# Graph convolutions of a four-layer graph network: table lookups by TensorE removed, every column gathered by GpSimd

## The chip, the core and the metric

One Trainium2 chip, one core of it. The time is the device time of one execution of the whole kernel, in microseconds (us). The kernel before takes 32684.31 us, the median of 3 runs (32668.05 to 32695.04).

## What is computed

Four graph layers run one after the other on 12500 nodes with 16 features and 400000 edges, sorted by destination: graph attention (two passes), a graph convolution network, a sheaf layer and a tensor-product layer. Each adds its result to `x` and normalises. The change touches the second layer, which aggregates over the edges twice:

```
def gcn_conv(x, edge_index, W, b, num_nodes):
    src, dst = (edge_index[0], edge_index[1])
    ...
    deg = segment_sum(ones, dst_f)
    dinv = where(deg > 0, rsqrt(deg), 0.0)
    norm = dinv[src_f] * dinv[dst_f]
    h = x @ W
    msg = h[src_f] * norm[:, None]
    out = segment_sum(msg, dst_f)
    return out + b

h = gcn_conv(x, edge_index, W1, b1, num_nodes)      # 16 -> 32 features
h = relu(batch_norm(h))
out = gcn_conv(h, edge_index, W2, b2, num_nodes)    # 32 -> 16 features
x = layernorm(x + out)
```

## The kernel before

The 400000 edges lie in 128 lanes of 3125 edges, one lane to a partition, and are worked in 25 chunks of 125 columns (`CH`). A column is one edge of each lane, so one column needs 128 rows of a node table, each at an index of its own. Nodes lie as 100 columns of 128 (`NT`).

Both aggregations of the graph convolution work on 16 features (the product with the weights stands after the first one and before the second), in the function `gcn_gather` (L935). Its two calls have the names `c1c` and `c2c`, made by `aggregate` in `gcn` (L2163 to L2171). Values are scaled by `dinv` and stored to a table in HBM (`tab16`, `tab16b`), and then, per chunk:

- **GpSimd** gathers columns 0 to 84 (`PCH` = 85) with one indirect DMA per column, 128 rows of 64 bytes, from the table into `G[b]`, one of two buffers (L494 in `gather_column_loop`). Ahead of a chunk it waits until the buffer was stored and the chunk's indices have landed, and then issues column after column without a wait.
- **TensorE and VectorE** look up columns 85 to 124 (`PC` = 40), ten batches of 4 columns (`NB`, `BE`), in the class `Match` (L1209). For a batch VectorE makes 13 one-hot masks of 128x512 (`heat`, L1269: is this index in this piece of the table), TensorE multiplies each mask with the piece of the table, in two parts for precision (L1278), VectorE keeps the right 16 of 128 rows (`mask`, L1288), TensorE sums them (`collapse`, L1298), and VectorE copies the result to `G` (`empty`, L1306). The indices of those columns were written once to HBM as numbers of two kinds by `match_rows` (L1169) at the start of the program; SyncE's queue loads them, spread over all partitions, 20 DMAs of 128 KB per chunk (L1258).
- Beside that a **side task** runs (`count_before_group`, L1074), which the sheaf layer needs later: 11 groups of 5 columns per chunk in `c1c`, 10 in `c2c`. Of each, VectorE makes two one-hot tiles (L1097, L1099), compares (`loT`, L1102), waits for TensorE's lookup (`pR`, L1127), and then multiplies, reduces and adds (L1105, L1107, L1108). ScalarE copies one 128x100 tile per group.
- At the end of a chunk VectorE waits for the gathered columns and runs 16 scans of 125 columns over `G` (L975), copies the last column to `carry` (L978), and SyncE loads the indices of the chunk after next (L501) and stores `G` to HBM (L1017).

The order on VectorE within a chunk is written by hand: masks of batch 0, then for each step `m` the `mask` of batch m-1, the masks of batch m+1, the side group m, and the `empty` of batch m-1. The last two groups have no masks ahead of them. The loop over chunks is a hardware loop over pairs of chunks with the last one behind it.

Elsewhere in the program the same `gather_column_loop` runs with all 125 columns: in the attention layer (`g1g_G`, `g2g_G`) beside other VectorE work, and in the sheaf layer (`se_G`). `extract` (L427) issues 4 times 25 indirect DMAs of the same kind behind each aggregation, with little beside them.

## Time and profile before

| | |
|---|---|
| median of 3 runs | 32684.31 us (32668.05 to 32695.04) |
| the profiled execution | 32672.44 us, its span 32670.6 us |
| busy, share of the span | PE 41%, PEld 32%, DVE 49%, ACT 8%, POOL 69% |
| stage `c1c`, from the first gather to the last scan | 11322 to 14779 us |
| stage `c2c` | 15144 to 18569 us |

DVE is VectorE, ACT ScalarE, POOL GpSimd, SP SyncE (SPq its DMA queue), PE TensorE's matmuls and PEld its weight loads. Times in the rows below are counted from the start of the span. A duration of a `DMA_INDIRECT` row is the time in which GpSimd issues the transfer, not that in which the data move. An idle time that ends by "issue" is one in which the engine waited for nothing that the profile shows.

### The profile page before, as it was taken

Reading aid. Unit: us, or ns where it says so; the run is one execution under the profiler, and the core shown is the slowest. Engines: PE = TensorE matmul, PEld = TensorE weight load, DVE = VectorE, ACT = ScalarE, POOL = GpSimd, SP = SyncE. Lnnn points to the kernel's source line nnn. Section 1 sums busy time; section 2 is a strip of 40 time slices with the busy share of each in tenths; the row PEclk is TensorE's granted clock in tenths of the full one; section 3 lists DMA queues with packets and bytes.
Section 4 is the critical chain, followed back from the end, with each engine's and each line's share of the span. In section 5 each row is a group of like instructions: output and inputs, shape, how many; then the busy total and the mean of one; then the engine's idle time right before and its main releaser. Section 6 shows DMA issues by size and latency. Waiting matters only on the chain. (4 is left out here: it accounts for less than half of the span.)

```text
span 32670.6 us, 266258 instructions
## 1 busy us (share of the span) xinstructions
PE 13491.3 (41%) x71326; PEld 10479.5 (32%) x71326; DVE 16103.5 (49%) x34560; ACT 2584.3 (8%) x3901; POOL 22511.4 (69%) x20275
## 2 busy tenths in 40 slices
PE   1111100211110177775777535444444441666663
PEld 1111100211110166664666423232323230454442
DVE  3434429344443677775777534444444443444442
ACT  0000000000000000000000001011111110333330
POOL 5777760477775288885888767777777774777772
PEclk5555555555555588886888756666666665777775
DMA  2111113111112311111111110000000002000001
GB/s 55 16 15 16 16 10 145 22 27 27 27 27 46 111 33 33 33 32 21 33 33 33 25 15 12 14 12 14 12 14 12 14 10 59 18 15 15 15 13 56
DMA packets 1117655, 946.20 MB, mean 29 GB/s; under 512 B 609084, under 2 KB 1060308, under 8 KB 1092308
## 3 DMA queue, kind: packets, MB, share of 16 engines
q1 hardware_dynamic: 468516, 706.27, 7.3%
q0 software_dynamic: 646368, 201.76, 6.4%
q10 hardware_dynamic: 1872, 28.29, 0.2%
q8 instruction: 307, 5.03, 0.1%
q14 instruction: 592, 4.85, 0.1%
HBM read 506.74 MB, written 428.17 MB: 29 GB/s over the span
## 5 line engine op out<-in xcount | busy, mean ns | idle before, releaser
L494 POOL DMA_INDIRECT g1g_G<-tab,g1g_stage x3125 | 3270.3, 1046 | 1237.8 <-issue 1025.7
L494 POOL DMA_INDIRECT se_G<-tab,se_stage x3125 | 3324.5, 1064 | 1085.3 <-issue 1072.5
L494 POOL DMA_INDIRECT g2g_G<-tab,g2g_stage x3125 | 2949.5, 944 | 1272.5 <-issue 1026.4
L1152 POOL DMA_INDIRECT messages<-pe_M,pe_rstage x2625 | 3178.9, 1211 | 905.3 <-issue 817.5
L1152 POOL DMA_INDIRECT messages<-se_M,se_rstage x2625 | 2980.1, 1135 | 865.7 <-issue 799.6
L494 POOL DMA_INDIRECT c2c_G<-tab16b,c2c_stage x2125 | 2769.4, 1303 | 856.0 <-issue 647.3
L494 POOL DMA_INDIRECT c1c_G<-tab,c1c_stage x2125 | 2761.3, 1299 | 793.7 <-issue 647.3
L1053 DVE SCALAR_TENSOR_TENSOR g2gh_junk<-g2gh_pB,g2gh_src_f,earlier 128x128 f32<-128x128 f32 (+4 forms) x2625 | 1453.7, 614 | 1951.3 <-POOLq L493 1928.0
L1567 PE MATMUL se_pTV<-ident,se_pair 128*32 128x128 f32 x3125 | 539.5, 313 | 4159.9 <-DVE se_pair L1474 4159.4
L739 PE MATMUL g1gh_acc<-g1gh_oh_hi,g1gh_oh_lo 128*128 128x100 bf16 x6250 | 539.0, 283 | 3746.7 <-DVE g1gh_oh_hi L719 3746.7
L1065 PE MATMUL g2gh_pB<-ident_b,src_lo 128*128 128x128 bf16 x2625 | 641.4, 286 | 3290.3 <-DVEq L1059 3249.5
L1278 PE MATMUL c1cm_acc<-c1cm_hot,c1cm_part 128*128 128x512 f32 x6500 | 1740.7, 429 | 344.3 <-DVE c1cm_hot L1269 344.3
L1278 PE MATMUL c2cm_acc<-c2cm_hot,c2cm_part 128*128 128x512 f32 x6500 | 1717.2, 425 | 400.9 <-DVE c2cm_hot L1269 400.9
L1567 PEld LDWEIGHTS se_pTV<-ident,se_pair 128*32 128x32 f32 x3125 | 283.8, 106 | 4534.9 <-issue 4486.2
L739 PEld LDWEIGHTS g1gh_acc<-g1gh_oh_hi,g1gh_oh_lo 128*128 128x128 bf16 x6250 | 508.6, 143 | 3777.1 <-DVE g1gh_oh_hi L719 3777.1
L717 DVE TENSOR_TENSOR g1gh_oh_lo<-dst_lo,iota 128x640 bf16<-128x640 f32 (+1 forms) x625 | 514.6, 823 | 2284.6 <-POOLq L493 2231.8
L1473 DVE COPY se_pair<-se_G 128x80 f32 (+1 forms) x625 | 139.9, 224 | 2888.7 <-DMA se_G<-tab,se_stage 2761.6
L1278 PEld LDWEIGHTS c1cm_acc<-c1cm_hot,c1cm_part 128*128 128x128 f32 x6500 | 1356.2, 213 | 640.7 <-issue 336.7
L1278 PEld LDWEIGHTS c2cm_acc<-c2cm_hot,c2cm_part 128*128 128x128 f32 x6500 | 1338.2, 210 | 691.3 <-issue 389.2
L1787 DVE TENSOR_TENSOR pe_outer<-pe_X,pe_A 128x640 f32 x625 | 520.9, 833 | 1941.8 <-PE pe_pT L1815 1855.5
L1065 PEld LDWEIGHTS g2gh_pB<-ident_b,src_lo 128*128 (+1 forms) x2625 | 278.4, 106 | 3433.3 <-issue 3187.5
L1822 PE MATMUL pe_pM<-p_wm,pe_outT 128*128 128x16 f32 x6250 | 905.2, 283 | 1034.6 <-ACT pe_outT L1849 1034.6
(607 smaller groups left out, 34105.5 us busy)
## 6 DMA issues: line engine op xcount, KB each, us to landing
scans<-g1w_W SPq DMA_DIRECT2D x25, 3187.5 KB, 10.0
c1cm_row<-match SPq DMA_DIRECT2D x500, 128.0 KB, 3.0
c2cm_row<-match SPq DMA_DIRECT2D x500, 128.0 KB, 3.0
edges<-g2g_G SPq DMA_DIRECT2D x25, 2062.5 KB, 6.8
g2w_G<-edges SPq DMA_DIRECT2D x25, 2062.5 KB, 11.6
scans<-g2w_W SPq DMA_DIRECT2D x25, 2062.5 KB, 7.3
g1g_G<-tab,g1g_stage POOLq DMA_INDIRECT x3125, 2.4
g2g_G<-tab,g2g_stage POOLq DMA_INDIRECT x3125
```

The costliest lines, as they stand in the source:

```text
L494: g.indirect_dma_start(out=G[b][:, t, :], out_offset=None, in_=table, in_offset=bass.IndirectOffsetOnAxis(ap=stage[b][:, t:t + 1], axis=0) ...
L717: v.tensor_tensor(oh_lo[o][b][:, part, :], bc(lo[:, at], [P, m, P], 2), bc(k.iota[:, :], [P, m, P], 1), ALU.is_equal).then_inc(ready, 1)
L739: mm = pe.matmul(acc[2 if o and direct else o][:, 0:NT], oh_lo[o][b][:, g, :], oh_hi[o][b][:, g, :], start=False, stop=True, skip_group_ch ...
L1053: ins = v.scalar_tensor_tensor(out=junk[g][:, :], in0=pB[b][:, a * GRP * P:(e + 1) * P], scalar=src_f[:, e:e + 1], in1=k.earlier[:, (GRP - ...
L1065: pe.matmul(pB[b][:, e * P:(e + 1) * P], k.src_lo[:, at].to_broadcast([P, P]), k.ident_b[:, :], start=True, stop=False)
L1152: g.indirect_dma_start(out=view, in_=M[b][:, DC + t, :], in_offset=None, out_offset=bass.IndirectOffsetOnAxis(ap=stage[b][:, t:t + 1], axis=0)
L1278: mm = pe.matmul(self.acc[m % 2][:, :], self.part[part][:, j * MR:(j + 1) * MR, :].rearrange("p r f -> p (r f)"), self.hot[m % 2][:, j, :] ...
L1473: ch(v.tensor_copy(pair[:, :, 0, :], G[b][:, at, 0:D]))
L1567: mm = pe.transpose(pT[:, g * P:(g + 1) * P], pair[:, g, :, :].rearrange("p n d -> p (n d)"), k.ident[:, :])
L1787: v.tensor_tensor(outer[:, :, :, :], bc(X[b][:, at, :], [P, GRP, D, DE], 3), bc(A[b][:, at, :], [P, GRP, D, DE], 2), ALU.mult).then_inc(ou ...
L1822: mm = pe.matmul(pM[:, g * D:(g + 1) * D], outT[:, g * P:(g + 1) * P], w[:, :], start=True, stop=True)
```

## The change

`gcn_gather` no longer uses `Match`. GpSimd gathers all 125 columns of a chunk, and SyncE's queue loads 125 indices per lane instead of 85. Gone are: the masks, `mask` and `empty` on VectorE, `multiply` and `collapse` on TensorE, the 20 loads of match rows per chunk on SyncE's queue, the preparation of the table's two parts (`vector_first`), and `match_rows` at the program's start. The side task, the scans and the stores stand as before. The line numbers of the functions behind the cut constants are 7 lower in the changed kernel up to `gcn_gather`.

```diff
--- before.py
+++ after.py
@@ -43,13 +43,6 @@
 XT = 25
 FULL, REST = N // P, N % P
 D = 16
-BE = 4
-PC = 40
-PARTS, PART_T = 2, mybir.dt.float32r
-NB = PC // BE
-PCH = CH - PC
-MR = P // D
-MJ = -(-NT // MR)
 H1, C1 = 3, 32
 C2 = 32
 HID = 64
@@ -932,45 +925,33 @@
                 over_chunks(a, chunk)
 
 
-def gcn_gather(k, name, table, values, left, scans, carry, side):
+def gcn_gather(k, name, table, scans, carry, side):
 
     with ExitStack() as st:
         c = Ctx(k.nc, st)
         G = [c.sb(f"{name}_G{b}", [P, CH, D]) for b in range(2)]
-        stage = [c.sb(f"{name}_stage{b}", [P, PCH], I32) for b in range(2)]
+        stage = [c.sb(f"{name}_stage{b}", [P, CH], I32) for b in range(2)]
         staged = [c.sem(f"{name}_staged{b}") for b in range(2)]
         got = [c.pool_dma_sem(f"{name}_got{b}") for b in range(2)]
         stored = [c.sem(f"{name}_stored{b}") for b in range(2)]
         scanned, step = c.sem(name + "_scanned"), c.sem(name + "_step")
         side = side(k, c, name + "h")
-        match = Match(k, c, name + "m", left)
         with k.nc.Block() as block:
             @block.gpsimd
             def _(g):
                 over_chunks(g, lambda i, b, j: gather_column_loop(
-                    g, i, j, b, table, G, stage, staged, stored, 16, got, PCH))
+                    g, i, j, b, table, G, stage, staged, stored, 16, got))
 
             @block.vector
             def _(v):
                 ch = Chain(v, step)
                 ch(v.memset(carry[:, 0:D], 0.0))
-                match.vector_first(v, ch, values)
                 side.vector_first(v)
 
                 def chunk(i, b, j):
-                    match.heat(v, i, 0)
-                    v.wait_ge(stored[b], (j + 1) * 16)
-                    for m in range(max(NB + 1, side.groups)):
-                        if 1 <= m <= NB:
-                            match.mask(v, i, m - 1)
-                        if m + 1 < NB:
-                            match.heat(v, i, m + 1)
-                        if m < side.groups:
-                            side.vector(v, ch, i, side.ranges[0][0] + m)
-                        if 1 <= m <= NB:
-                            match.empty(v, G[b], i, m - 1)
-                    v.wait_ge(match.emptied, (i + 1) * NB + 2)
-                    v.wait_ge(got[b], (j + 1) * (16 * PCH))
+                    for m in range(side.groups):
+                        side.vector(v, ch, i, side.ranges[0][0] + m)
+                    v.wait_ge(got[b], (j + 1) * (16 * CH))
                     for f in range(D):
                         ch.loose(v.tensor_tensor_scan(G[b][:, :, f], k.keep_d[:, cols(i)], G[b][:, :, f],
                                                       carry[:, f:f + 1], ALU.mult, ALU.add))
@@ -982,19 +963,12 @@
 
             @block.tensor
             def _(pe):
-                match.tensor_first(pe)
                 side.tensor_first(pe)
 
                 def chunk(i, b, j):
-                    for m in range(max(NB + 1, side.groups)):
-                        if m < side.groups:
-                            side.tensor_rows(pe, i, side.ranges[0][0] + m)
-                        if m < NB:
-                            match.multiply(pe, i, m)
-                        if 1 <= m <= NB:
-                            match.collapse(pe, i, m - 1)
-                        if m < side.groups:
-                            side.tensor(pe, i, side.ranges[0][0] + m, False)
+                    for m in range(side.groups):
+                        side.tensor_rows(pe, i, side.ranges[0][0] + m)
+                        side.tensor(pe, i, side.ranges[0][0] + m, False)
                 over_chunks(pe, chunk)
 
             @block.scalar
@@ -1005,24 +979,19 @@
             def _(s):
                 for b in range(2):
                     s.sem_inc(stored[b], 16)
-                    load_indices(s, k.src_lanes, stage, staged, b, b, 0, PCH)
-
-                def chunk(i, b, more=True, index=True):
+                    load_indices(s, k.src_lanes, stage, staged, b, b)
+
+                def chunk(i, b, more=True):
+                    s.wait_ge(scanned, i + 1)
                     if more:
-                        for m in range(NB):
-                            match.reload(s, i, m)
-                    s.wait_ge(scanned, i + 1)
-                    if index:
-                        load_indices(s, k.src_lanes, stage, staged, i + 2, b, 0, PCH)
+                        load_indices(s, k.src_lanes, stage, staged, i + 2, b)
                     s.dma_start(rows(scans)[:, cols(i), :], G[b][:, :, :]).then_inc(stored[b], 16)
-                for m in range(NB):
-                    match.load(s, 0, m)
                 with s.Fori(0, PAIRS - 1) as j:
                     chunk(2 * j, 0)
                     chunk(2 * j + 1, 1)
                 chunk(NCH - 3, 0)
-                chunk(NCH - 2, 1, True, False)
-                chunk(NCH - 1, 0, False, False)
+                chunk(NCH - 2, 1, False)
+                chunk(NCH - 1, 0, False)
                 s.wait_ge(stored[0], 16 * (PAIRS + 2))
                 s.wait_ge(stored[1], 16 * (PAIRS + 1))
 
@@ -1164,147 +1133,6 @@
                 s.dma_start(k.rank_lanes.rearrange("p (i c) -> p i c", c=CH)[:, :, DC:CH],
                             k.rank[:, :].rearrange("p (i c) -> p i c", c=CH)[:, :, DC:CH]).then_inc(stored, 16)
                 s.wait_ge(stored, 16)
-
-
-def match_rows(k, name):
...
-class Match:
...
 class DirectSums:
@@ -1907,7 +1735,6 @@
         k.lanes = k.dram("lanes", [P, 51])
         k.spread_buf = k.dram("spread_buf", [SPREAD_SIZE])
         scan16 = k.dram("scan16", [E + P, D])
-        k.match = [k.dram(f"match{h}", [NCH, PC * P], F16) for h in range(2)]
         k.carried = k.dram("carried", [P + 1, 51])
         tab16 = k.dram("tab16", [NP, D])
         tab16b = k.dram("tab16b", [NP, D])
@@ -1925,7 +1752,6 @@
                 k.dst_i = Ctx(nc, s0).sb("dst_i", [P, LANE], I32)
                 setup(k, x, src, dst)
                 digits(k, "ds", k.src_i, k.src_lo, k.src_hi)
-            match_rows(k, "mr")
             with ExitStack() as s2:
                 k.h2 = Ctx(nc, s2).sb("h2", [P, NT, C2 + 2])
                 gat1(k, w, dst, carry, first, y)
@@ -2165,7 +1991,7 @@
             vector_block(k, name + "a", lambda v, ch: ch(v.tensor_tensor(
                 xs[:, :, :], values, bc(dinv[:, :], [P, NT, D], 2), ALU.mult)))
             store_nodes(k, name + "b", [xs[:, :, :]], table)
-            gcn_gather(k, name + "c", table, xs[:, :, :], agg, scan16, carry, side)
+            gcn_gather(k, name + "c", table, scan16, carry, side)
             lane_carries(k, name + "d", carry[:, 0:D], D, k.by_dst, ALU.add, scan16)
             extract(k, name + "e", scan16, k.by_dst, agg, D, ALU.add)
 
```

On VectorE, at the start of the first loop over chunks of `c1c`. The one-hot masks and `kept` belong to `Match`, the other rows to the side task. Before, without rows that only set registers:

```order
L1269 TENSOR_SCALAR c1cm_hot<-c1cm_row,c1cm_first 128x512 x13
...
L1097 TENSOR_TENSOR c1ch_oh_lo<-src_lo,iota 128x640
...
L1099 TENSOR_TENSOR c1ch_oh_hi<-src_hi,iota 128x500
...
L1102 TENSOR_SCALAR c1ch_loT<-c1ch_pB,part 128x640
L1105 TENSOR_TENSOR c1ch_prod<-c1ch_pR,c1ch_oh_hi 128x500
...
L1107 TENSOR_REDUCE c1ch_r<-c1ch_prod 128x5
...
L1108 TENSOR_TENSOR rank<-c1ch_r,rank 128x5
...
L1288 SCALAR_TENSOR_TENSOR c1cm_kept<-c1cm_row,c1cm_slot,c1cm_acc 128x512
L1269 TENSOR_SCALAR c1cm_hot<-c1cm_row,c1cm_first 128x512 x13
```

and now:

```order
L1066 TENSOR_TENSOR c1ch_oh_lo<-src_lo,iota 128x640
...
L1068 TENSOR_TENSOR c1ch_oh_hi<-src_hi,iota 128x500
...
L1071 TENSOR_SCALAR c1ch_loT<-c1ch_pB,part 128x640
L1074 TENSOR_TENSOR c1ch_prod<-c1ch_pR,c1ch_oh_hi 128x500
...
L1076 TENSOR_REDUCE c1ch_r<-c1ch_prod 128x5
...
L1077 TENSOR_TENSOR rank<-c1ch_r,rank 128x5
```

The groups of the side task now follow each other with nothing between them.

On GpSimd, the whole of the gather of `c1c`: the loop body with two chunks, and the last chunk behind it. Before:

```order
L93 ISA
L494 DMA c1c_G<-tab,c1c_stage 128x16 x170
L93 REGISTER_ALU
L93 COMPARE_AND_BRANCH
L494 DMA c1c_G<-tab,c1c_stage 128x16 x85
```

and now:

```order
L86 ISA
L487 DMA c1c_G<-tab,c1c_stage 128x16 x250
L86 REGISTER_ALU
L86 COMPARE_AND_BRANCH
L487 DMA c1c_G<-tab,c1c_stage 128x16 x125
```

Nothing else was moved between these rows; a pair of chunks now has 250 indirect DMAs in place of 170.

## Rows read from the trace of the kernel before

**Rows 1.** Groups of instructions: busy us, mean ns of one, idle before, releaser
```profile
L494 POOL DMA_INDIRECT g1g_G<-tab,g1g_stage x3125 | 3270.3, 1046 | 1237.8 <-issue 1025.7 <-DMA g1g_stage<-in_src_dram 212.1
...
L494 POOL DMA_INDIRECT g2g_G<-tab,g2g_stage x3125 | 2949.5, 944 | 1272.5 <-issue 1026.4 <-DMA g2g_stage<-in_src_dram 246.1
L494 POOL DMA_INDIRECT c2c_G<-tab16b,c2c_stage x2125 | 2769.4, 1303 | 856.0 <-issue 647.3 <-DMA c2c_stage<-in_src_dram 208.7
L494 POOL DMA_INDIRECT c1c_G<-tab,c1c_stage x2125 | 2761.3, 1299 | 793.7 <-issue 647.3 <-DMA c1c_stage<-in_src_dram 146.4
...
L717 DVE TENSOR_TENSOR g1gh_oh_lo<-dst_lo,iota 128x640 bf16<-128x640 f32 (+1 forms) x625 | 514.6, 823 | 2284.6 <-POOLq L493 2231.8 <-issue 47.4 <-DVE carry L817 4.6
...
L719 DVE TENSOR_TENSOR g1gh_oh_hi<-dst_hi,iota 128x500 bf16<-128x500 f32 (+1 forms) x625 | 419.6, 671 | 0.0
```

**Rows 2.** Waits in stage c1c: total us, times, longest us
```profile
POOL c1c_G L494 <- issue: 647.3, 2124, 0.3
DVE c1ch_prod L1105 <- PE c1ch_pR L1127: 622.6, 275, 5.2
```

**Rows 3.** Tiles c1c_G, then c2c_G: min/median/max ns, first and last start us
```profile
L494 POOL DMA_INDIRECT c1c_G<-tab,c1c_stage x2125: 940/947/8802, 11322.2 to 14729.9; - x194
L978 DVE COPY carry<-c1c_G x25: 174/176/383, 11467.5 to 14778.6; 128x16 f32<-128x16 f32 x25
L494 POOL DMA_INDIRECT c2c_G<-tab16b,c2c_stage x2125: 940/947/8406, 15144.2 to 18560.0; - x194
L978 DVE COPY carry<-c2c_G x25: 174/175/386, 15294.6 to 18568.4; 128x16 f32<-128x16 f32 x25
```

**Rows 4.** Timeline of c1c where masks are made: start us, us, instruction
```profile
12021.21 10.44 DVE L1269 TENSOR_SCALAR c1cm_hot<-c1cm_row,c1cm_first 128x512 fp32r<-128x512 f16 x26 [0.22 <-DVE carry L978]
12024.17 7.61 POOL L494 DMA_INDIRECT c1c_G<-tab,c1c_stage  x1 [0.31 <-issue]
...
12044.71 0.82 DVE L1097 TENSOR_TENSOR c1ch_oh_lo<-src_lo,iota 128x640 bf16<-128x640 f32 x1
12045.22 1.72 POOL L494 DMA_INDIRECT c1c_G<-tab,c1c_stage  x1 [0.30 <-issue]
```

**Rows 5.** Timeline of c1c, a group without masks, then the scans
```profile
12144.91 0.84 DVE L1097 TENSOR_TENSOR c1ch_oh_lo<-src_lo,iota 128x640 bf16<-128x640 f32 x1
12145.68 0.67 DVE L1099 TENSOR_TENSOR c1ch_oh_hi<-src_hi,iota 128x500 bf16<-128x500 f32 x1
12146.15 1.02 POOL L494 DMA_INDIRECT c1c_G<-tab,c1c_stage  x1 [0.30 <-issue]
...
12151.88 6.03 DVE L975 TENSOR_TENSOR_SCAN c1c_G<-keep_d,carry,c1c_G 128x125 f32<-128x125 f32 x16
12153.82 1.18 POOL L494 DMA_INDIRECT c1c_G<-tab,c1c_stage  x1 [0.30 <-issue]
```

**Rows 6.** Windows without masks, POOL's gathers alone: 8 of c1c, 5 of c2c, summed
```profile
sum 133.50, POOL 102.22; mean POOL 12.78
sum 24.80, POOL 19.04; mean POOL 3.81
```

**Rows 7.** Windows, stages c1c and g1g: us, busy (x) by engine, PEclk, DMA share, GB/s
```profile
11320.00:14780.00 3460.00, 2605.36 (x14002) 2257.45 (x14002) 2711.07 (x5834) 69.92 (x276) 2761.33 (x2125) 0.82 0.16 32
...
215.00:4510.00 4295.00, 539.45 (x6253) 508.77 (x6253) 1737.60 (x2623) 0.00 (x0) 3268.90 (x3124) 0.53 0.13 22
```

**Rows 8.** Timeline of GpSimd in the extraction behind c1c, 23 columns in a row
```profile
14811.40 0.94 POOL L427 DMA_INDIRECT c1e_gs<-scan,c1e_si  x1 [0.30 <-issue]
...
14838.88 0.94 POOL L427 DMA_INDIRECT c1e_gs<-scan,c1e_si  x1 [0.30 <-issue]
```

**Rows 9.** Timeline, the last gather of stage c2c
```profile
18559.97 0.94 POOL L494 DMA_INDIRECT c2c_G<-tab16b,c2c_stage  x1 [0.30 <-issue]
```

**Rows 10.** Timeline of VectorE, first instruction of match_rows and first behind it
```profile
43.41 1.20 DVE L1190 CAST mr_src_f<-src_i 128x1000 f32<-128x1000 int32 x1 [0.52 <-PEq L305]
...
69.96 0.14 DVE L1987 MEMSET g_w1d<- 48x96 f32 x1 [6.20 <-remote]
```

118 lines of the change are left out of this document (removed).

## The prediction

> **What bounds the kernel now.** The stages run one after the other, so only the two gathers of the graph convolution and `match_rows` can move by themselves. I read the groups of instructions first, then the waits inside stage `c1c`, then its timeline.
>
> The first thing to see is that GpSimd hardly rests in either gather. Its 2125 gathers of `c1c` are busy 2761.3 us, and every gap between two of them is "issue", 0.3 us at most [rows 1, 2]. It runs from 11322.2 to about 14730.8, in 3409 us [rows 3]. VectorE ends its last chunk at 14778.6, with a period of (14778.6 - 11467.5)/24 = 138.0 us per chunk against GpSimd's 3409/25 = 136.4 [rows 3]. So before the change the two sides of the stage are level: VectorE, which also waits 622.6 us for TensorE's lookup [rows 2], is ahead as the bound by under 2 us per chunk.
>
> The second thing is that GpSimd's 85 columns are not cheap there. One gather is 1299 to 1303 ns in these stages, 944 ns in `g2g` [rows 1]. The timeline shows the cause: a gather that falls beside 26 back-to-back masks takes 7.61 us, and one beside the one-hot tile behind 13 masks takes 1.72 us [rows 4]. The median is 947 ns, the maximum 8802 [rows 3]; a few gathers pay for all. Per chunk the excess is (1299 - 944) x 85 = 30 us.
>
> **What a column costs without the masks.** The clean rate: 22 columns that follow each other in the extraction take 14838.88 - 14811.40 = 27.48 us, 1.249 us each [rows 8], which is 0.944 of issue and 0.304 of gap (647.3/2124) [rows 2]. The same 0.944 stands over 3125 gathers of `g2g` [rows 1].
>
> On top comes what the remaining VectorE work takes. Beside `oh_hi` and `loT` a gather takes 1.02 us, beside the scans 1.18 us [rows 5]. Over 16 groups without masks of `c1c`, 133.5 us, GpSimd is busy 102.22: the idle 31.28 at 0.304 are 103 columns, whose clean issue would be 97.1, so 5.1 us are excess, 0.32 per group. Over five groups of `c2c` the same working gives 5.76/0.304 = 18.9 columns, 17.9 clean, 1.15 of excess, 0.23 per group [rows 6]. The third source agrees: `g1g` has 50 pairs of such tiles per chunk and (1046 - 944) x 125 = 12.8 us of excess, 0.26 per pair [rows 1]. The 16 scans run 6.03 us and stretch some three gathers by 0.24 each [rows 5]: 0.7 us.
>
> Per chunk that makes 11 x 0.32 + 0.7 = 4.2 us in `c1c` and 10 x 0.23 + 0.7 = 3.0 us in `c2c`, on top of 125 x 1.249 = 156.1.
>
> **The change part by part.**
> - Gathers, `c1c`: GpSimd starts at 11322.2 as before (the first index load has 125 instead of 85 columns, no matter). 3125 x 1.249 = 3903 and 25 x 4.2 = 105 bring it to 15330. The end of the stage lies behind the last gather: in `c2c` before, it ended at 18559.97 + 0.94 and the copy to `carry` at 18568.4 + 0.17, 7.7 us later [rows 3, 9]. So 15338, against 14778.7: **+559 us**.
> - Gathers, `c2c`: 15144.2 + 3903 + 75 + 7.7 = 19130, against 18568.6: **+561 us**.
> - Masks, `mask`, `empty`, `multiply`, `collapse`, the preparation of the table and 500 loads of match rows per stage: nothing of it stands on the new critical path, which is GpSimd alone. Its only worth there is that the gathers run cleanly again, and that is in the rate above. VectorE's share of a chunk falls to the side groups and the scans. A group without masks is 6.97 us from its `oh_lo` to the scans [rows 5], with `kept` and `empty` still in it, so a chunk is 11 x 7 + 6.5 = 84 us, beside 160 us of gathering. That is the cover of the side task: 76 us per chunk to spare. SyncE's queue loses its waits for `kept`; index load and store then wait only for `scanned`, a chunk ahead of when GpSimd wants them, some 150 us.
> - `match_rows` goes: VectorE's first instruction of it starts at 43.41, the next stage's at 69.96, nothing beside it [rows 10]: **-26.5 us**.
> - Between the stages nothing changes in kind.
>
> Sum: 559 + 561 - 26.5 = +1094 us on the profiled execution's 32672, so 33766. The median of the runs stands 12 us above that execution; against it I forecast **33770 us**, 3.3% slower.
>
> **Ends of the range.** What I don't know is the excess on 125 columns when side groups follow each other. Its lowest value is none (the rate of `g2g`), 180 us less: 33590. Its highest near value is that each group costs what one does behind the masks, 1.72 - 0.94 = 0.78 us [rows 4]: 11 x 0.78 + 0.7 = 9.3 per chunk, 5.1 more than priced, over 50 chunks 255 us more: 34020. A gain is excluded for this term, since the minimum of all 2125 gathers is 940 ns [rows 3]. I take the values in between because three stretches without masks agree on 0.23 to 0.32. Range: 33590 to 34020.
>
> **A rule weighed.** In `g1g` the one-hot tiles occupy VectorE for some 2 x (514.6 + 419.6) = 1868 us (the pair of `dst` and the like pair of `src`), 75 us per chunk, and cost the gathers 12.8 us [rows 1]: 0.17 us per us of such work, not one for one. Per side group, 1.49 us of tiles give 0.25. The Trainium skill (SBUF — State Buffer, "SBUF: two separate sides") calls the port pair that VectorE and GpSimd share an exclusive lock, held for the whole instruction by a VectorE instruction in a two-port mode or with two SBUF inputs, while the other is fully blocked. By that rule the sum would be that of rival 2, 34670, instead of 33770. For the masks it points the right way (the 7.61 us gather [rows 4]); for the tiles it is too dear by the rows.
>
> **Rivals.**
> 1. *The excess per column of `g1g` holds.* There VectorE makes tiles all the time, and a column costs 0.102 us over the clean issue; it would be 12.8 us per chunk instead of 3.0 to 4.2, 640 in place of 180: 34230. For it: both are the same tiles and the same 125 columns. Against it: 100 tiles per chunk there, 20 to 22 here. 5%.
> 2. *Tiles and scans block GpSimd for their whole length.* 11 x 1.49 + 6.0 = 22.4 and 10 x 1.49 + 6.0 = 20.9 us per chunk, 1083 in place of 180: 34670. Against it stand the scans of 6.03 us, beside which gathers still come out in 1.18 [rows 5], and the 75 us of tiles per chunk of `g1g` that cost 12.8 [rows 1]. 3%. (It is the lock of the Trainium skill's SBUF page, taken literally.)
> 3. *The side task becomes the bound.* TensorE's granted clock is 0.82 in `c1c` and 0.53 in `g1g`, where it has less to do [rows 7]; near 0.5 it works at the lower of its two levels, 1.2 GHz, and each group would wait longer for `pR`. The longest such wait now is 5.2 us, the mean 622.6/275 = 2.3 [rows 2]. From 14 us per group on, twice today's 7, a chunk of `c1c` would pass 160 us; at 15 it would be 171.5 and the kernel 285 us slower than forecast, 34055. 2%.
> 4. *The other side: the gathers get cheaper than clean.* Issue might today wait for the DMA engines, which 20 loads of 128 KB per chunk on SyncE's queue share with it. The kernel comes out not slower only when a column costs under 1.249 - 1094/6250 = 1.074 us. If a quarter of the 0.944 went, a column would be 1.013 and the kernel 6250 x 0.236 = 1475 us faster than forecast, 32295. Against it: with no such load about, in the extraction and in `g2g`, issue is 0.94 all the same [rows 1, 8]. 1%.
>
> **Chances.** The forecast with its range has 0.88; the rivals 0.05, 0.03, 0.02 and 0.01; 0.01 is left for what I don't see. All but the fourth end over 0.2% slower (about what a measurement of this kernel can tell from no change). So slower 0.98, within 0.2% 0.01, faster 0.01. The range leaves out rivals 1, 2 and 4 and little else.
>
> **What would show each step.** In the groups: `c1c_G` and `c2c_G` with 3125 gathers each at 965 to 985 ns and no row of `c1cm_` or `c2cm_`. In the tiles: the maximum of a gather under 2 us, a span of about 4008 us in `c1c` and 3978 in `c2c`. In the waits: VectorE's largest wait of the stage is for the gather's DMA, 25 times some 75 us; GpSimd waits only for "issue". In the windows: TensorE's clock at 0.5 to 0.6. Wrong would be: gaps of GpSimd that end by a store or an index load (the buffers bound it); gathers beside `oh_lo` and `oh_hi` of over 2 us (rivals 1 and 2); VectorE with no wait for the gather at a chunk's end (rival 3); gathers under 900 ns (rival 4).

## The result: 4.3% slower, and the profile after

The changed kernel takes **34096.87 us** (median of 4 runs, 34084.25 to 34101.07) against 32686.44 (32668.05 to 32695.04) for the kernel before: ratio 1.0432 [1.0414, 1.045]. The forecast was 33770, its range 33590 to 34020. Direction and bound were right; 327 us were missing.

The groups of the changed kernel, costliest first (busy us, mean ns of one, idle before and its releaser); line numbers are the changed kernel's:

```profile
L487 POOL DMA_INDIRECT g1g_G<-tab,g1g_stage x3125 | 3276.7, 1049 | 1208.9 <-issue 1025.4 <-DMA g1g_stage<-in_src_dram 183.5
...
L487 POOL DMA_INDIRECT c1c_G<-tab,c1c_stage x3125 | 3110.3, 995 | 1170.3 <-issue 1024.6 <-DMA c1c_stage<-in_src_dram 145.8
L487 POOL DMA_INDIRECT c2c_G<-tab16b,c2c_stage x3125 | 3079.1, 985 | 1233.4 <-issue 1024.7 <-DMA c2c_stage<-in_src_dram 208.7
```

They answer to [rows 1]. A gather is down from 1299 and 1303 ns to 995 and 985, now that the masks, beside which [rows 4] had the dearest, are gone. There are 1000 more of them per stage. The idle time by "issue" is 1024.6 over 3124 gaps, 0.328 each, where [rows 2] had 0.305.

The tile `c1c_G`, then `c2c_G` (min/median/max ns, first and last start), against [rows 3]:

```profile
L487 POOL DMA_INDIRECT c1c_G<-tab,c1c_stage x3125: 938/944/1557, 11300.8 to 15434.8; - x196
L959 DVE COPY carry<-c1c_G x25: 174/175/176, 11471.6 to 15443.3; 128x16 f32<-128x16 f32 x25
L487 POOL DMA_INDIRECT c2c_G<-tab16b,c2c_stage x3125: 938/944/1547, 15806.5 to 19909.4; - x196
L959 DVE COPY carry<-c2c_G x25: 174/175/384, 15977.1 to 19917.8; 128x16 f32<-128x16 f32 x25
```

The waits of stage `c1c` (total us, times, longest), against [rows 2]:

```profile
DVE c1c_G L956 <- DMA c1c_G<-tab,c1c_stage: 2088.8, 25, 91.8
POOL c1c_G L487 <- issue: 1024.6, 3124, 3.3
DVE c1ch_prod L1074 <- PE c1ch_pR L1096: 699.5, 275, 2.6
```

GpSimd alone bounds the stage: VectorE waits 84 us per chunk for the gathers, GpSimd never waits for a buffer. But one thing is new in that view: the longest wait by "issue" was 0.3 us, and now is 3.3. The windows of both stages, columns as in [rows 7], show TensorE at a granted clock of 0.50 and 0.51, its lower level of 1.2 GHz, with nothing on the path:

```profile
11300.00:15445.00 4145.00, 935.28 (x5495) 857.85 (x5495) 1204.80 (x2074) 69.58 (x275) 3110.35 (x3125) 0.50 0.09 13
15806.00:19920.00 4114.00, 850.16 (x4995) 779.95 (x4995) 1109.55 (x1924) 63.25 (x250) 3079.14 (x3125) 0.51 0.09 13
```

**Two costs that the sum lacked or had too small** are seen in the timeline of `c1c` (start us, us, instruction). First, GpSimd at the 113th and 114th gather of a chunk:

```profile
12107.01 0.94 POOL L487 DMA_INDIRECT c1c_G<-tab,c1c_stage  x1 [0.31 <-issue]
12108.25 0.94 POOL L487 DMA_INDIRECT c1c_G<-tab,c1c_stage  x1 [0.30 <-issue]
12112.35 0.94 POOL L487 DMA_INDIRECT c1c_G<-tab,c1c_stage  x1 [3.15 <-issue]
12113.60 0.94 POOL L487 DMA_INDIRECT c1c_G<-tab,c1c_stage  x1 [0.30 <-issue]
```

Each of the 25 chunks has exactly one such gap, of 3.1 to 3.3 us, ahead of its 114th gather. It is no property of the change: the kernel before has it in its three gathers of 125 columns, 25 times in each. Second, two side groups that follow each other, with the gathers between them:

```profile
12141.83 0.82 DVE L1066 TENSOR_TENSOR c1ch_oh_lo<-src_lo,iota 128x640 bf16<-128x640 f32 x1 [0.24 <-DVE rank L1077]
12141.96 1.51 POOL L487 DMA_INDIRECT c1c_G<-tab,c1c_stage  x1 [0.30 <-issue]
12142.57 0.67 DVE L1068 TENSOR_TENSOR c1ch_oh_hi<-src_hi,iota 128x500 bf16<-128x500 f32 x1
...
12148.63 0.83 DVE L1066 TENSOR_TENSOR c1ch_oh_lo<-src_lo,iota 128x640 bf16<-128x640 f32 x1 [0.24 <-DVE rank L1077]
12148.77 1.50 POOL L487 DMA_INDIRECT c1c_G<-tab,c1c_stage  x1 [0.30 <-issue]
```

The groups come every 6.80 us, and each one's `oh_lo` starts 0.13 us ahead of a gather, which then takes 1.50 us. Five clean gathers take 5 x 1.249 = 6.245 us; with 0.55 of excess they take the same 6.80. Where groups follow each other VectorE's period is 6.80 us all along (median 6.803), and the gathers fall into step with it; why is told below, with e16. In the kernel before, [rows 5] had one group without masks behind masks, at a phase of its own.

Where the time went, trace against trace (us, from starts and lengths in the timelines):

| stretch | before | after | difference | forecast |
|---|---|---|---|---|
| start to first gather of `c1c` | 11322.2 | 11300.8 | -21.4 | -26.5 |
| `c1c`, first gather to end of last copy to `carry` | 3456.6 | 4142.6 | +686.1 | +559 |
| between the two | 365.5 | 363.1 | -2.4 | 0 |
| `c2c`, the same | 3424.3 | 4111.4 | +687.1 | +561 |
| all behind it | 14102.0 | 14173.9 | +71.9 | 0 |

The five differences sum to the spans' 34091.9 - 32670.6 = 1421.3.

### The profile page after: what moved, and what is told of

Same layout as the page of the kernel before. It is cut to its first block and busy times, and to the rows that moved or that the text cites. A ratio compares the mean times of both kernels' runs of the same rounds, so it can differ in the third digit from the quotient of the medians.

```text
span 34091.9 us, 220370 instructions
## 1 busy us (share of the span) xinstructions
PE 10210.6 (30%) x54301; PEld 7718.8 (23%) x54301; DVE 13094.5 (38%) x27031; ACT 2583.6 (8%) x3901; POOL 23222.9 (68%) x22275
## 5 line engine op out<-in xcount | busy, mean ns | idle before, releaser
L487 POOL DMA_INDIRECT c2c_G<-tab16b,c2c_stage x3125 | 3079.1, 985 | 1233.4 <-issue 1024.7
L487 POOL DMA_INDIRECT c1c_G<-tab,c1c_stage x3125 | 3110.3, 995 | 1170.3 <-issue 1024.6
L1096 PE MATMUL c1ch_pR<-c_free_place,c1ch_loT 128*128 128x100 f32 x2750 | 674.1, 432 | 3116.3 <-DVE c1ch_loT L1071 3116.3
L1096 PE MATMUL c2ch_pR<-c_free_place,c2ch_loT 128*128 128x100 f32 x2500 | 613.0, 432 | 3164.8 <-DVE c2ch_loT L1071 3164.8
L1096 PEld LDWEIGHTS c1ch_pR<-c_free_place,c1ch_loT 128*128 128x128 f32 x2750 | 606.0, 329 | 3189.4 <-DVE c1ch_loT L1071 3189.4
L1096 PEld LDWEIGHTS c2ch_pR<-c_free_place,c2ch_loT 128*128 128x128 f32 x2500 | 551.0, 329 | 3231.1 <-DVE c2ch_loT L1071 3231.1
L1650 PEld LDWEIGHTS pe_pM<-p_wm,pe_outT 128*128 128x128 f32 x6250 | 894.3, 219 | 1326.4 <-ACT pe_outT L1677 1246.6
```

The lines of the kernel that those rows point to most:

```text
L487: g.indirect_dma_start(out=G[b][:, t, :], out_offset=None, in_=table, in_offset=bass.IndirectOffsetOnAxis(ap=stage[b][:, t:t + 1], axis=0) ...
L1096: mm = pe.matmul(pR[:, g * NT:(g + 1) * NT], loT[:, g, :], table[:, :], start=True, stop=True)
L1650: mm = pe.matmul(pM[:, g * D:(g + 1) * D], outT[:, g * P:(g + 1) * P], w[:, :], start=True, stop=True)
```

## The experiments

Sixteen runs of twelve kernels stand here; four are repeats on another chip or a second time, and two are the kernels before and after as they are. Letters name theories: **S**, the gap belongs to more than 113 gathers in a row on one semaphore; **A**, it belongs to a run of gathers without a wait; **L**, the excess per group comes from the step between groups and gathers, not from the amount of VectorE's work; **M**, the stages behind got slower because buffers moved in HBM. The runs e1 to e10 fell on a chip on which VectorE, TensorE and ScalarE stood still for tens of us at a time (ScalarE for up to 56) in every trace, and the kernel before took 39.3 ms in place of 32.7. So their times say nothing on GpSimd's costs, and only gaps and durations are read from them. The runs e11 to e17 fell on two others. There the kernel before took 32549 us beside e11 to e13 and 32693 beside e14 to e17; the changed kernel took 34097 beside 32686 and 34099 beside 32549, so its variants are set against those two. It was not run on the chip of e14 to e17, and why the kernel before differs by 144 us from chip to chip, where the changed one doesn't, is open.

### Where the gap comes from

**e1_wait_mid** and **e2_wait_early**: a wait, already fulfilled, in the middle of the gathers of `c1c` and `c2c`.

```diff
     for t in range(count):
+        if pause is not None and t == pause:      # 63 in e1, 8 in e2
+            g.wait_ge(staged[b], (j + 1) * 16)
+            g.nop(nofuse=True)
```

Expected of e1: 

> In the changed kernel every chunk of 125 gathers has one gap of 3.1 to 3.3 us ahead of its 114th gather, where the others are 0.305. Here one wait that is met already (for the chunk's indices, again) and a nop stand ahead of the 64th gather of each chunk of both graph convolution stages. Theory A, the gap comes of more than 113 gathers in a row without a wait: all 50 gaps go, both stages get 25 x 2.9 = 72 us shorter (the waits themselves cost under 0.2 us each), and the kernel 135 to 145 us shorter than the changed kernel's 34097, near 33955. Theory B, the gap comes of the place in the code (an instruction fetch) or of something that counts on over chunks: the gaps stay, at the same or another place, and the time stays within 20 us.

Expected of e2: 

> As the run with a wait in the middle of a chunk, but the wait stands ahead of the 9th gather, so that 117 gathers follow it. Theory A (a count since the last wait of GpSimd): the gap stays but moves by 8, ahead of the 122nd gather of a chunk, and the time is that of the changed kernel. If the count began at the chunk's start or at the loop's, the gap stays ahead of the 114th. If any wait at all in a chunk removed it, it would be gone and both stages 72 us shorter.

41475.22 us (ratio 1.052 [1.0454, 1.0587]) and 41213.48, beside 39393.83 for the kernel before. The gap stays ahead of the 114th gather, 25 times per stage, in both. A falls. The attention layer's gathers, which have one more semaphore instruction every 5 columns, have it there too. From e1, the 113th and 114th gather of a chunk:

```profile
15056.13 0.94 POOL L490 DMA_INDIRECT c1c_G<-tab,c1c_stage  x1 [0.30 <-issue]
15060.18 0.94 POOL L490 DMA_INDIRECT c1c_G<-tab,c1c_stage  x1 [3.10 <-issue]
```

**e4_cols85**: only columns 0 to 84 are gathered; the other 40 are left out (zeros stand in `G`).

```diff
-                    g, i, j, b, table, G, stage, staged, stored, 16, got))
+                    g, i, j, b, table, G, stage, staged, stored, 16, got, 85))
```

Expected: 

> Leaves out the gathers of columns 85 to 124 of both graph convolution stages (those columns are zeroed once and not looked up in any way), so the output is not the reference's. Theory, the stage is the sum of its gathers: no long gap (85 is under 113), a chunk takes 85 x 1.249 plus the excess by VectorE, which the changed kernel shows as 6.4 us in c1c and 5.1 in c2c, so 112.6 and 111.3 us per chunk and 2816 and 2782 us from the first gather on. Against the 136.4 of the kernel before, with as many gathers, that is what the masks cost GpSimd: 24 us per chunk. Rival, the side task bounds a chunk once the gathers are short: VectorE would have no wait for the gather at a chunk's end, and the period would be 84 us or more by its own work; at 112 us it should still wait some 30 us per chunk.

39281.28 us. No gap inside any chunk; the only long ones are at chunk starts, where GpSimd waits for the store of the buffer, which stands behind VectorE's chunk end (848.5 us in `c1c`). So the gap needs more than 85 gathers. The expected 112.6 us per chunk can't be judged here: this chip's VectorE bounds the stage.

**e7_reversed**: the columns are issued from 124 down to 0.

```diff
-    for t in range(count):
+    for t in (reversed(range(count)) if back else range(count)):
```

Expected: 

> A wait in the middle or near the start of a chunk left the long gap of GpSimd (3.2 us) ahead of the 114th gather, so it is no count since the last wait and, as the code had grown by two instructions, no fixed place in the code. Here the 125 columns of a chunk of both graph convolution stages are gathered from the last to the first. Theory C, the gap belongs to the operand (column 113 of the index tile or of the buffer): it moves ahead of the 13th gather issued. Theory E, it is a count of gathers since the chunk began: it stays ahead of the 114th issued. Times as for the changed kernel in both cases.

40742.9 us (before 39298.81). The gap is ahead of the 114th gather issued, column 11, and not of column 113: it goes by the count, not by the operand.

**e8_two_sems**: columns 0 to 62 count on one semaphore, 63 to 124 on a second one, in `c1c` and `c2c`; VectorE waits for both.

```diff
-                             ).then_inc(got[b], 16)
+                             ).then_inc((late if late and t >= 63 else got)[b], 16)
...
-                    v.wait_ge(got[b], (j + 1) * (16 * CH))
+                    v.wait_ge(got[b], (j + 1) * (16 * 63))
+                    v.wait_ge(late[b], (j + 1) * (16 * (CH - 63)))
```

Expected: 

> The first 63 gathers of a chunk count up one semaphore, the other 62 a second one, in both graph convolution stages; VectorE waits for both. Theory S, the gap comes of more than 113 gathers in a row on one semaphore: it goes, 25 gaps in each stage, and each stage is 72 us shorter than in the changed kernel (4143 and 4112 us from first gather to the last copy to carry). If the count is of gathers whatever their semaphore, the gap stays ahead of the 114th and the times stay.

40953.32 us. The gaps are gone from both stages, and stay in the three gathers left as they were. S holds: 125 gathers on one semaphore have the gap, 85 don't, and 63 and 62 on two don't. GpSimd's instructions are the same in number and order, so their place in the code is not it either.

**e11_after_all_sems** has that edit in all five gathers, **e12_after_again** is the changed kernel itself, for the same chip.

Expected of e11: 

> The changed kernel with columns 63 to 124 of every chunk on a second semaphore in all five gathers. Theory S (the gap comes with more than 113 gathers in a row on one semaphore, and is on the path of the stages that GpSimd bounds): no gap of over 1 us inside a chunk in any of the five; the two convolution gathers each 60 to 75 us shorter than in the unaltered changed kernel, the two of the attention layer by up to as much where GpSimd bounds them, the sheaf layer's not at all; 130 to 290 us in all. Rival (the gap lies beside a wait for VectorE at the chunk's end anyway on this chip): gap gone, time within 60 us of the unaltered one.

Expected of e12: 

> The changed kernel itself, unaltered, on the chip on which its variants ran, so that they have it to be set against. No theory hangs on it alone. By the stages of its trace: GpSimd's gap of 3.1 to 3.3 us ahead of the 114th gather in each of the 25 chunks of both convolution gathers; a period of 6.80 us and an excess of 0.50 to 0.55 us where side groups follow each other (phase lock). If it shows neither, both are properties of the variants and not of the change. Time: between 40700 and 41300 us on this chip, from the variants with one edit each (40743 to 41213).

e12: 34098.73 us (34091.6 to 34146.29), ratio 1.0474 [1.0456, 1.0491] to the kernel before. e11: 33727.11 (33714.81 to 33732.01), ratio 1.0361 [1.0343, 1.0378]; **372 us less** than e12, and more than the 130 to 290 expected. (e12's own time was expected at 40700 to 41300, for the chip of e1 to e10; it has the gap and the step as expected.) The groups of e11:

```profile
L487 POOL DMA_INDIRECT c1c_G<-tab,c1c_stage x3125 | 3113.3, 996 | 1097.9 <-issue 952.1 <-DMA c1c_stage<-in_src_dram 145.8
L487 POOL DMA_INDIRECT c2c_G<-tab16b,c2c_stage x3125 | 3089.5, 989 | 1160.7 <-issue 952.1 <-DMA c2c_stage<-in_src_dram 208.6
```

The gathers are as long as ever, and the idle time by "issue" is down from 1024.6 to 952.1: 72.5 us, which is 25 x 2.9. That is the cost of the gap per stage. It was expected of four stages; the sheaf layer's gather, of which nothing was expected, took 7858 us and had taken 7939 in the changed kernel's first trace, 81 more. Its gathers and scatters follow each other on GpSimd, so it is on the path there as well. Five stages of 72.5 us make 363; e11 also has shorter turns in the product layer (27 us, see below), so the sum fits only roughly.

### What the step between groups and gathers costs

**e5_pad**, its repeat **e5b_pad**, and on the other chip **e16_pad_alone**: one more copy on VectorE per side group, whose result is not used. More work makes the period longer, 7.52 us, near six clean gathers (7.49).

```diff
         ch(v.tensor_reduce(r5[:, :], prod[:, :, :], axis=AX.X, op=ALU.add))
+        ch(v.tensor_copy(pad[:, 0:500], pR[:, 0:500]))
```

Expected of e5: 

> Adds one VectorE copy of 128x500 from PSUM to SBUF, about 0.7 us, to every side group of both stages; it reads no SBUF tensor. In the changed kernel a group takes 6.8 us and meets five gathers, 5 x 1.249 = 6.25; the trace shows nearly every group's one-hot tile starting just behind the start of a gather, which takes 1.5 us instead of 0.94. Theory L, the two engines are locked in step: the excess per group is what is missing between the group's length and a whole number of gathers, 0.55. With 7.5 us per group, six gathers (7.49) fit, the excess falls to 0.1 or less, and both stages get shorter by about 11 x 25 x 0.4 = 110 and 10 x 25 x 0.35 = 90 us, though work was added. Theory F, a one-hot pair costs a fixed 0.5 us whatever its place: the stages stay as they are within 15 us. Theory H, more VectorE work means more excess: they get longer.

Expected of e5b: 

> The kernel with one VectorE copy from PSUM of 0.7 us more in each side group, again, since the chip of its first run held VectorE and TensorE up for some 27 us at a time in every kernel, which hid what was asked. As then: theory L (the engines are locked in step; a group of 7.5 us fits six gathers) says an excess of 0.1 us or less per group and stages about 110 and 90 us shorter than the changed kernel's 4143 and 4112; theory F (a fixed 0.5 us per one-hot pair) says no change within 15 us; theory H says longer.

Expected of e16: 

> The changed kernel with one more VectorE copy of 128x500 per side group, from the accumulator in PSUM to SBUF; what it computes is not used. Theory L (the groups run in step with the gathers, so that each group's first tile falls on the start of a gather): period 7.52 us, six gathers, excess per group about 0.1 us in place of 0.55 and 0.47; that is 11 x 0.45 + 10 x 0.37 = 8.7 us for the two convolutions' chunks together, 25 x 8.7 = 215 us off the changed kernel's 34099, to about 33880, although VectorE does more. Rival (the excess comes from the amount of VectorE work): no gain, or slower than 34099.

e5: 41928.95 us, ratio 1.0635 [1.0532, 1.0739]; e5b: 41933.31, 1.067 [1.0484, 1.0856]; in both the mean gather is 953 to 955 ns. That proves little: on that chip, e1, e2, e7 and e8 without the copy had 970 to 982 in `c1c` and 956 to 958 in `c2c`, and the stages did not get shorter as expected, since VectorE bounded them. e16 gives the time: **33854.94 us** (33849.65 to 33869.1), 244 less than e12, ratio 1.0359 [1.0343, 1.0375]. Its groups, and two groups' starts in its timeline:

```profile
L487 POOL DMA_INDIRECT c1c_G<-tab,c1c_stage x3125 | 2992.5, 958 | 1169.8 <-issue 1024.0 <-DMA c1c_stage<-in_src_dram 145.8
L487 POOL DMA_INDIRECT c2c_G<-tab16b,c2c_stage x3125 | 2986.6, 956 | 1233.3 <-issue 1024.6 <-DMA c2c_stage<-in_src_dram 208.7
```

```profile
12335.78 0.68 DVE L1078 COPY c1ch_pad<-c1ch_pR 128x500 f32<-128x500 f32 x1
...
12336.99 0.88 DVE L1067 TENSOR_TENSOR c1ch_oh_lo<-src_lo,iota 128x640 bf16<-128x640 f32 x1 [0.24 <-DVE rank L1079]
12337.01 0.94 POOL L487 DMA_INDIRECT c1c_G<-tab,c1c_stage  x1 [0.30 <-issue]
12337.79 0.67 DVE L1069 TENSOR_TENSOR c1ch_oh_hi<-src_hi,iota 128x500 bf16<-128x500 f32 x1
12338.26 1.02 POOL L487 DMA_INDIRECT c1c_G<-tab,c1c_stage  x1 [0.30 <-issue]
...
12344.56 0.89 DVE L1067 TENSOR_TENSOR c1ch_oh_lo<-src_lo,iota 128x640 bf16<-128x640 f32 x1 [0.24 <-DVE rank L1079]
12344.59 0.94 POOL L487 DMA_INDIRECT c1c_G<-tab,c1c_stage  x1 [0.30 <-issue]
...
12777.11 0.94 POOL L487 DMA_INDIRECT c1c_G<-tab,c1c_stage  x1 [0.30 <-issue]
12777.68 0.82 DVE L1067 TENSOR_TENSOR c1ch_oh_lo<-src_lo,iota 128x640 bf16<-128x640 f32 x1 [0.24 <-DVE rank L1079]
12778.36 0.96 POOL L487 DMA_INDIRECT c1c_G<-tab,c1c_stage  x1 [0.30 <-issue]
```

L holds. The busy time of the gathers falls by 117.8 us in `c1c` and 92.5 in `c2c`, 210 together, where 215 were expected; the rest of the 244 lies behind these stages, which the edit doesn't touch (the sheaf gather takes 7910 us in place of 7939). The same tiles cost 0.08 us (1.02 - 0.94) where the gather starts 0.02 to 0.03 us behind `oh_lo`, and 0.56 where it starts 0.13 behind it. In the first case `oh_lo` itself takes 0.88 in place of 0.82 and the groups come every 7.57 us; in most groups of e16 the period is 7.52 us, a gather starts 0.57 ahead of `oh_lo` and the next one takes 0.96 or 0.97, as in the last three rows. The excess in step is what is left of VectorE's period over whole gathers: 6.80 - 5 x 1.249 = 0.56 there, 7.52 - 6 x 1.249 = 0.03 here.

Why they fall into step is seen in the changed kernel's trace, where now and then a gather starts later beside the tiles:

```profile
11803.69 0.82 DVE L1066 TENSOR_TENSOR c1ch_oh_lo<-src_lo,iota 128x640 bf16<-128x640 f32 x1 [0.26 <-DVE carry L959]
11804.31 1.03 POOL L487 DMA_INDIRECT c1c_G<-tab,c1c_stage  x1 [0.30 <-issue]
11804.43 0.67 DVE L1068 TENSOR_TENSOR c1ch_oh_hi<-src_hi,iota 128x500 bf16<-128x500 f32 x1
...
12303.32 0.82 DVE L1066 TENSOR_TENSOR c1ch_oh_lo<-src_lo,iota 128x640 bf16<-128x640 f32 x1 [3.13 <-issue]
12303.56 1.40 POOL L487 DMA_INDIRECT c1c_G<-tab,c1c_stage  x1 [0.30 <-issue]
12304.06 0.67 DVE L1068 TENSOR_TENSOR c1ch_oh_hi<-src_hi,iota 128x500 bf16<-128x500 f32 x1
```

These gathers start 0.62 and 0.24 us behind `oh_lo`, those in step 0.13, and all end 1.64 or 1.65 us behind its start, 0.23 us behind the end of `oh_hi`. In that trace it is so for all 456 gathers of both stages that start 0.07 to 0.66 us behind `oh_lo` (0.22 to 0.24 us behind the end of `oh_hi`). So such a gather is held until `oh_hi` is done, and where it ends no longer hangs on where it began. From that end the next starts can be counted: the gap and four clean gathers bring the next one beside tiles to 1.64 + 0.30 + 4 x 1.249 - 6.80 = 0.14 us behind the next `oh_lo`, where it is held again. With the period of e16 and five clean gathers it is 1.64 + 0.30 + 5 x 1.249 - 7.52 = 0.67 us (0.68 in the last row of e16 above), so late that hardly anything of `oh_hi` is left to wait for.

**e10_all_sems_pad** and, on the other chip, **e17_all_sems_pad**: both edits in the changed kernel.

Expected of e10: 

> The changed kernel with both finds: two semaphores per chunk in all five gathers of 125 columns, and the VectorE copy of 0.7 us more per side group of the graph convolutions. Theories S and L together: 125 x 2.9 = 363 us and some 11 x 25 x 0.44 + 10 x 25 x 0.37 = 213 us off the changed kernel's 34097, so 33520, a ratio to the kernel before of 1.026; the five stages have no gap over 0.4 us within a chunk, the gathers of both graph convolutions 952 ns or less. That is still slower than before, since 2000 gathers more at 1.249 us are 2498 us and the lookups that they replace took as long as the gathers beside them. Without L (a fixed price per one-hot pair): 33730.

Expected of e17: 

> Both edits in the changed kernel: second semaphore in all five gathers and the extra copy per side group. If the two costs are separate terms they add: 371 us (measured for the semaphores alone) and 215 us (expected for the copy alone), so about 33510, still slower than the kernel before by about 3%, since 80 more columns of GpSimd at 1.249 us in each pair of chunks remain. Rival (they overlap): over 33600.

e10: 42032.84 us, ratio 1.0687 [1.06, 1.0773]: no gain to be seen, since VectorE bounded the stages there (GpSimd waits 1576 us for the store of its buffer in `c1c`). e17: **33462.86 us** (33452.12 to 33470.66), ratio 1.024 [1.0225, 1.0256], 636 less than e12; the single edits gave 372 and 244, together 616. From the first gather to the last, `c1c` and `c2c` are 132 us shorter in e11 than in the changed kernel's first trace, 211 in e16 (together 343) and 360 in e17. So the two costs are separate terms and add.

### The stages behind, and a version that beats both

**e13_dram_kept**: the changed kernel with the removed lookup's HBM buffers still laid out.

```diff
+        k.match = [k.dram(f"match{h}", [NCH, 40 * P], F16) for h in range(2)]
```

Expected: 

> The changed kernel with the two HBM buffers of the removed lookup (k.match) still laid out and never used, so that every buffer behind them lies at the address it had before the change. Theory M (what is behind the second convolution got 72 us longer because its tables and scans moved in HBM): the scatter of the sheaf layer and its matrix products are back near 1135 and 594 ns, and from the last gather of the second convolution to the end of the span it takes some 70 us less than in the unaltered kernel of the same call. Rival (it is the clock or the instruction layout): no difference beyond the scatter between two executions of one kernel. Gathers and gaps of the convolution unchanged in both.

34092.73 us, ratio 1.0472 [1.0455, 1.049]: 6 us from e12, inside its runs. The scatter of the sheaf layer takes 1150 ns. M falls.

**e14_before_again**: the kernel before, a second trace.

Expected: 

> The kernel before, unaltered, for a second trace of it. Open is why everything behind the second convolution took 72 us longer in the changed kernel. If that belongs to the change, the sheaf gather takes 7891 us and the rest 5820 again, with a mean of 1135 ns for the sheaf layer's scatter and 407 us of waits for its one-hot tiles. Rival (one execution differs so from another): 7920 or more and 1145 ns or more.

32705.12 us, with 1136 ns for that scatter. The rows of the sheaf layer's scatter, of e14 and of the changed kernel:

```profile
L1152 POOL DMA_INDIRECT messages<-se_M,se_rstage x2625 | 2982.7, 1136 | 865.4 <-issue 799.6 <-DVE se_M L1533 65.8
```

```profile
L1121 POOL DMA_INDIRECT messages<-se_M,se_rstage x2625 | 3022.8, 1152 | 865.0 <-issue 799.6 <-DVE se_M L1361 65.4
```

Two traces of the one kernel against three of the other (1150 to 1161 ns) say that the difference belongs to the program and not to one execution. From the first gather of the sheaf layer to its last it takes 7891 and 7893 us in two traces of the kernel before, 7939, 7963 and 7944 in three of the changed one. Some 40 us of it are these scatters; what stretches them is not shown. In e16, whose edit is in the convolution alone, they take 1139 ns, nearly as before the change. In the product layer behind it, GpSimd's idle time at every second turn of a chunk, where the hardware loop turns, is 4.7 to 5.2 us after the change and 2.5 before. Eleven turns make some 27 us:

```profile
28324.87 1.23 POOL L1152 DMA_INDIRECT messages<-pe_M,pe_rstage  x1 [2.52 <-issue]
```

```profile
29728.95 2.79 POOL L1121 DMA_INDIRECT messages<-pe_M,pe_rstage  x1 [5.18 <-issue]
```

(the first of the kernel before, the second of the changed one, the first of these turns in each). In e11 and e17 that idle time is back at 2.5, although they only change semaphores; in e12, e13 and e16 it is not. So it goes with the build. What of a build sets it was not found, and no further kernel was tried for it.

**e9_before_two_sems**, and **e15_before_two_sems** on the other chip: the kernel before with the second semaphore in its three gathers of 125 columns.

Expected of e9: 

> The kernel before, with its lookups by TensorE, and the semaphore changed after 63 of 125 gathers in the three stages that gather all 125 columns (both attention gathers and the sheaf layer). Theory S (a long gap of 3.2 us once more than 113 gathers in a row count up one semaphore) says: 25 gaps of each of the three stages go, 75 x 2.9 = 218 us, and the kernel comes to 32470 us where the kernel before takes 32686, a ratio of 0.993; where another engine ends the chunk, less. If the gaps were hidden, the ratio is 1.000.

Expected of e15: 

> The kernel before with columns 63 to 124 of the 125-column gathers (both of the attention layer and the sheaf layer's) on a second semaphore, once more. On a chip whose VectorE and TensorE are not held up, by theory S: both attention gathers 60 to 75 us shorter and, as the changed kernel with the same edit showed, the sheaf gather about 80 shorter; 200 to 220 us in all, so 0.993 to 0.994 of the kernel before, which would beat both kernels. Rival (the convolution stages, which VectorE bounds by a hair, take it back): there is no coupling between stages, so none of it should be lost; a ratio above 0.997 would speak for this.

e9: 39152.54 us, ratio 0.9956 [0.9918, 0.9994], where 0.993 was expected. e15: **32536.89 us** (32528.06 to 32543.41) against 32693.02 (32641.96 to 32697.93) for the kernel before, ratio 0.9956 [0.9942, 0.9969]. It is 0.4% faster than the kernel before on the same chip, the only version that is, though 156 us are less than the 200 to 220 expected. Its waits in `g2g`:

```profile
POOL g2g_G L494 <- issue: 952.1, 3124, 0.3
```

The two attention gathers gave 54 and 75 us against e14, about as expected. The sheaf gather gave 25 in place of 80: its gaps by "issue" fell by 54 us, but its scatter rose from 1136 to 1146 ns, 26 us.

## Why the prediction was wrong in size and right in kind

The measured 34096.87 lies 77 us above the range. The steps that failed are terms of the sum: the gap per gather, sized at 0.304 us and 0.328 in fact; the excess per side group, sized at 0.32 and 0.23 us and 0.55 and 0.47 in fact; and the stages behind, put at nothing, where 72 us came. None of the four rivals came; this was the 0.01 left for what was not seen, where the range had been given 0.88.

**Held.** GpSimd is the only bound of both stages; VectorE waits 25 times for the gather (84 and 89 us, forecast "some 75"); TensorE's clock is at 0.50; the longest gather is 1.56 us, under 2; no row of `Match` is left; the minimum of a gather is 938 ns, nothing cheaper than clean. The gathers of `c1c` were forecast at 965 to 985 ns and take 995; `c2c`'s take 985. The buffers never made GpSimd wait.

**Failed, by their steps.**

1. *"The clean rate: ... 1.249 us each", times 125.* The rate was read over 22 columns in a row and the gap of 0.304 over chunks of 85. In chunks of 125 the mean gap is 0.328. The missing 2.9 us per chunk are 72 us per stage, 145 in all; e11 showed 72.5 in each. The number stood in [rows 1]: `g1g` and `g2g`, with 125 columns, have 1025.7 and 1026.4 us of "issue", 0.328 per gap, and the waits of `c1c` have 647.3/2124 = 0.305 [rows 2]. I took `g2g`'s 0.944 as the like case and its gap from another.
2. *"0.32 per group" and "0.23 per group".* Both came from groups without masks behind masks. Groups that follow each other cost 0.55 in `c1c` and 0.47 in `c2c`, since they are in step with the gathers. The scans, priced at 0.7, cost 0.9 (four gathers in place of three). The mean gathers give 125 x (995 - 944) = 6.4 and 125 x (985 - 944) = 5.1 us per chunk in place of 4.2 and 3.0: +54 and +53 us. Groups behind the scans, which are not in step, cost 0.2 on average (0.23 and 0.22) in the changed kernel, near the figures read. The upper end of 0.78 would have covered this term alone. (Redone with `c2c`'s own numbers that end is 34035, which changes nothing.)
3. *"Between the stages nothing changes in kind."* True up to `c2c` (-2.4), but behind it the kernel is 72 us slower, by the two places above. This had no range at all.
4. *`match_rows`, -26.5.* It gave 21.4: 5 us.

The four make 145 + 107 + 72 + 5 = 329, less the 2 between the stages: the missing 327. The end of the range, 34020, held 255 us for step 2 and nothing for 1 and 3. That the direction came out is no luck: 2000 more gathers at 1.249 us on an engine that was level with the bound before; the 127 and 126 us missing per stage change the size and not the sign.

**The rivals.** The first (the excess of `g1g` per column) wanted 12.8 us per chunk, and 6.4 and 5.1 came; the third (side task as the bound) fell, a group takes 6.80 us and not 14; the fourth fell. The second, the full lock, wanted 22.4 us per chunk. The gather beside 1.49 us of one-hot tiles is 0.56 us longer in one phase and 0.08 or 0.03 in another, and never more than 0.62 (1557 ns). The Trainium skill (SBUF — State Buffer, "SBUF: two separate sides") has the shared port pair go for the whole instruction to whichever starts first, and names a VectorE instruction with two SBUF inputs only against a GpSimd one that reads SBUF; the other is blocked. The trace agrees in that a gather held by `oh_hi` ends at a fixed 0.23 us behind that tile's end. It does not agree with the rival's reading, that the whole 1.49 us are lost per group: a gather that starts 0.02 us behind `oh_lo` is not lengthened by it. An estimate from the rows: a gather minds the tiles only about 0.71 us after its start (0.94 less the 0.23), and the price is what is then left of `oh_hi`.

## What to carry to other kernels

When a stage is rebuilt in the form that another stage has, take the whole of that stage's rate, busy time and idle time, and compare the mean gap with the longest one: a rare gap of 3 us hides in a mean of 0.328. When two engines that disturb each other run with fixed periods, do not carry over a price measured at random phase; ask how many whole steps of the one fit into the period of the other, and what is left over; better still, look whether the one ends at a fixed moment of the other, for from there the phase can be counted. And an issue-bound GpSimd loop can be tested cheaply by spreading its transfers over two semaphores.

## What the runs showed of the hardware

- GpSimd, issuing indirect DMAs that all count on one semaphore, stops once for 3.0 to 3.6 us (over all traces) ahead of the 114th. It doesn't depend on the column, on a wait between, or on the semaphore's value, which goes on rising from chunk to chunk; it is not there with 85 or 63 in a row. With the second semaphore the changed kernel takes 372 us (1.1%) less and the one before 156 less. What in the chip does it is open; so is the exact count for other kinds of transfers.
- More work on VectorE made the kernel faster: 525 more copies of 0.68 us, 244 us less, 210 of them in the gathers beside it. A gather's issue that starts 0.07 to 0.66 us behind a 128x640 one-hot tile ends 0.23 us behind the end of the 128x500 one that follows, wherever it started (456 of 456); one that starts 0.02 us behind costs nothing itself. So 0.1 us of shift makes 0.5 us of difference, and two engines with fixed periods lock into a phase, dear or cheap.
- Stages that a change does not touch moved by 72 us of 14100, and most of it goes with the build: GpSimd's idle time at eleven turns of a hardware loop is 2.5 us in four kernels (before, e11, e15, e17) and 4.7 to 5.2 in three (changed, e13, e16). What sets it is open.
